# Macaron block in one pipelined kernel: the first channel mix takes x^T from DRAM and normalises it by columns, in a new instruction order

## What is computed

```python
x = x + 0.5 * channel_mix(layernorm(x))      # FFN1
x = x + retention(layernorm(x))              # RET, 8 heads of 32, state carried over the tokens
x = x + 0.5 * channel_mix(layernorm(x))      # FFN2, the same weights

def channel_mix(x):
    x_prev = x shifted by one token, zero in front
    xr = mu_r * x + (1 - mu_r) * x_prev
    xk = mu_k * x + (1 - mu_k) * x_prev
    return sigmoid(xr @ W_r) * (relu(xk @ W_k) ** 2 @ W_v)
```

## Time and profile before

| | us |
|---|---|
| median of 3 runs (lowest, highest) | 339.76 (339.11, 339.87) |
| the profiled execution's own time | 338.8 |
| its span in the trace | 336.9 |
| TensorE busy | 322.3 |
| VectorE busy | 297.0 |
| ScalarE busy | 210.5 |
| GpSimd busy | 135.1 |

### The profile page before, as it was taken

One profiled execution on the slowest core, in us unless ns is written; L12 is line 12 of the kernel. 1 busy time (PEld: TensorE's weight loads), 2 busy tenths in 40 slices (PEclk: granted clock), 3 DMA queues, 4 the chain that ended last, 5 costly groups with the idle time before them and its releaser, 6 DMA issues.

```text
span 336.9 us, 11291 instructions
## 1 busy us (share of the span) xinstructions
PE 322.3 (96%) x4260; PEld 302.4 (90%) x4260; DVE 297.0 (88%) x696; ACT 210.5 (62%) x422; POOL 135.1 (40%) x242
## 2 busy tenths in 40 slices
PE   4979999999999999999999999999999999999975
PEld 4869899999999999999899999989999998989874
DVE  4989899999999999899999989999897979888954
ACT  2877556775757586674758567475857555374362
POOL 4386165608163451706245270715424154221130
PEclk9999999999999999999999999999999999999999
DMA  7610010102001020201102020100000010000001
GB/s 232 247 35 31 4 34 0 34 5 62 4 2 63 2 65 3 65 2 27 41 3 64 2 63 2 53 16 32 2 19 17 2 35 7 26 4 31 34 2 62
DMA packets 11556, 12.08 MB, mean 36 GB/s; under 512 B 1008, under 2 KB 11120, under 8 KB 11504
## 3 DMA queue, kind: packets, MB, share of 16 engines
q1 hardware_dynamic: 11072, 11.18, 10.4%
q10 hardware_dynamic: 432, 0.20, 0.2%
HBM read 7.18 MB, written 4.19 MB: 34 GB/s over the span
## 4 chain that ended last, share of the span: by engine, by line
PE 88%; DVE 4%; issue 3%; ACT 2%; POOL 1%; DMA 1%; ACTq 0%; DVEq 0%; POOLq 0%
PE psum L964 39%; PE psum L956 24%; PE psum L948 7%; PE psum L1035 5%; PE psum L1067 5%; PE psum L1054 3%; PE psum L1025 2%; PE psum L1080 2%; PE psum L1157 1%; DMA ident<-in_ident 1%; ACT xn L344 1%; DVE stats L624 1%; PE psum L1161 1%; PE psum L1127 1%; PE psum L1115 0%
## 5 line engine op out<-in xcount | busy, mean ns | idle before, releaser
L199 POOL TENSOR_TENSOR xr_lo<-xrT,xr_hi 128x512 fp32r<-128x512 f32 x24 | 41.1, 1728 | 99.8 <-ACT xr_hi L375 99.8
L344 ACT ACTIVATE xn<-x,shift,rstd 128x256 f32<-128x256 f32 x96 | 52.0, 591 | 10.1 <-POOL shift L283 10.1
L692 DVE TENSOR_TENSOR attn<-psum,decay 128x512 f32<-128x512 f32 x64 | 42.4, 683 | 4.7 <-PE psum L1035 4.7
L964 PE MATMUL psum<-w_hi,xr_hi 128*128 128x256 f32 x124 | 38.6, 312 | 1.7 <-DVE xr_lo L199 1.2
L624 DVE BATCH_NORM_STATS2 stats<-x 128x6 f32<-128x256 f32 x96 | 35.7, 414 | 4.9 <-DMA x<-in_x 4.6
L276 POOL TENSOR_TENSOR var_eps<-moments,eps 128x2 f32<-128x2 f32 x48 | 18.9, 395 | 43.7 <-DVE moments L628 42.9
L964 PE MATMUL psum<-w_hi,ka_hi 128*128 128x256 f32 x120 | 35.7, 297 | 0.7 <-ACT rgate L403 0.7
L956 PE MATMUL psum<-xa_hi,w_hi 128*128 128x256 f32 x128 | 35.8, 280 | 0.0
L956 PE MATMUL psum<-xk_hi,w_hi 128*128 128x256 f32 x120 | 34.5, 288 | 1.1 <-POOL xk_lo L193 0.9
L956 PE MATMUL psum<-xa_lo,w_hi 128*128 128x256 f32 x128 | 35.5, 278 | 0.0
L956 PE MATMUL psum<-xa_hi,w_lo 128*128 128x256 f32 x128 | 35.5, 277 | 0.0
(11 more groups left out here) (105 smaller groups left out, 1043.4 us busy)
## 6 DMA issues: line engine op xcount, KB each, us to landing
x<-in_x SPq DMA_DIRECT2D x15, 256.0 KB, 2.9
x_out<-y SPq DMA_DIRECT2D x15, 256.0 KB, 3.1
w_f<-in_w SPq DMA_DIRECT2D x7, 256.0 KB, 5.9
decay<-in_decay SPq DMA_DIRECT2D x1, 512.0 KB, 6.6
decq<-in_decq SPq DMA_DIRECT2D x1, 256.0 KB, 6.1
deck<-in_deck SPq DMA_DIRECT2D x1, 256.0 KB, 6.2
x_out<-y SPq DMA_DIRECT2D x2, 128.0 KB, 1.8
x<-in_x ACTq DMA_DIRECT2D x1, 128.0 KB, 2.8
```

The source lines that it names most:

```text
L199: engine.tensor_tensor(xr_lo[f][n % 2][:], xrT[f][n % 2][:], xr_hi[f][n % 2][:].bitcast(F32), ALU.subtract).then_inc(xr_lo_ready[f], 1)
L344: act.activation(xn[s][n % 2][:, t, :], x[n % len(x)][:, t, :], ACT.Identity, bias=shift[s][n % 2][:, t:t + 1], scale=rstd[s][n % 2][:, t: ...
L692: dve.tensor_tensor(attn[r][:], bank[B_SCORES[r]].rearrange("p (g c i) -> p g c i", g=G, c=TILES), decay[:, r, :, :].unsqueeze(2).broadcas ...
L964: mm = pe.matmul(halves(b)[:, t, :], xt[:, g, cols], wt[:, g, :], start=(j == 0), stop=(j == 5))
```

## The change

From block 3 on (`FIRST_ROWS`), the first mix no longer transposes. The host hands over x^T (256 x 4096) as a further input. Per block, SP loads a 256x256 piece of it into `xT` (two buffers), with channels on partitions. `rstd` and `shift` now lie side by side in `scale_shift`, per token on the partitions. SP stores them to a DRAM scratch, 16 bytes for each of 128 partitions, and loads all 512 numbers of the block back into every partition (`rows`, 2 KB each). GpSimd multiplies `xT` by the row of `rstd` and adds the row of `shift`, two operations of 128x512, in place in `xnT`.

```diff
+            def load_xT(n):
+                k = n - FIRST_ROWS
+                sp.wait_ge(xT_scaled, max(k - 1, 0))
+                sp.dma_start(xT[n % 2][:], xT_groups[:, :, n * BT:(n + 1) * BT]).then_inc(xT_loaded[n % 2], 16)
+
+            def store_rows(n):
+                sp.wait_ge(shift_ready[FFN1], shifts(FFN1, n + 1))
+                sp.dma_start(rows_blocks[n], scale_shift[FFN1][n % 2][:].rearrange("p k t -> p (k t)")).then_inc(rows_stored[n % 2], 16)
+
+            def load_rows(n):
+                k = n - FIRST_ROWS
+                sp.wait_ge(rows_stored[n % 2], 16 * stored_rows(n))
+                sp.wait_ge(xnT_ready[FFN1], FIRST_ROWS + k - 1 if k > 1 else 0)
+                sp.dma_start(rows[n % 2][:].rearrange("q p k t -> q (p k t)"), rows_io[2 * n * BT:2 * (n + 1) * BT].partition_broadcast(P)).then_inc(rows_loaded[n % 2], 16)
...
+            def by_token(row):
+                return row.rearrange("q p t -> q t p").unsqueeze(1).broadcast_to([P, G, TILES, P])
+            def scale_xT(n):
...
+                pool.tensor_tensor(tokens(xnT[FFN1][n % 2][:, :, 1:BT + 1]), tokens(xT[n % 2][:]), by_token(rows[n % 2][:, :, 0, :]),
+                                   ALU.mult).then_inc(xT_scaled, 1)
+            def shift_xT(n):
+                pool.wait_ge(xT_scaled, n - FIRST_ROWS + 1)
+                normal = tokens(xnT[FFN1][n % 2][:, :, 1:BT + 1])
+                pool.tensor_tensor(normal, normal, by_token(rows[n % 2][:, :, 1, :]), ALU.add).then_inc(xnT_ready[FFN1], 1)
```

`dT` is not formed for these blocks. ScalarE scales the block by mu (`scale_k` into `akT`, `scale_r` into `arT`, two operations of 128x256 each), and VectorE adds (1 - mu) * x_prev in the operation it had:

```diff
+            def scale_k(f, n):
+                halo(f, n)
...
+                for g in range(G):
+                    act.activation(akT[n % 2][:, g, :], xnT[f][n % 2][:, g, 1:BT + 1], ACT.Copy, scale=mu[:, 1, g:g + 1]).then_inc(ak_ready, 1)
...
+                if f == FFN1 and n >= FIRST_ROWS:
...
+                    for g in range(G):
+                        dve.scalar_tensor_tensor(out=xkT[f][n % 2][:, g, :], in0=xnT[f][n % 2][:, g, 0:BT], scalar=mu_rest[:, 1, g:g + 1],
+                                                 in1=akT[n % 2][:, g, :], op0=ALU.mult, op1=ALU.add).then_inc(xk_ready[f], 1)
+                    return
```

Three blocks (FFN1 0, RET 0, FFN2 15: `FAST`) are normalised by VectorE as (x - mean) * rstd, and of `inverse_std` only the power stays on GpSimd:

```diff
+            def normalize_fast(s, n, x):
+                dve.wait_ge(rstd_ready[s], n + 1)
+                dve.wait_ge(xnT_psum[s], max(n - 1, 0))
+                for t in range(TILES):
+                    dve.tensor_scalar(xn[s][n % 2][:, t, :], x[n % len(x)][:, t, :], moments[s][n % 2][:, t, 0:1],
+                                      rstd[s][n % 2][:, t:t + 1], ALU.subtract, ALU.mult).then_inc(xn_ready[s], 1)
```

The warm-up reads a tile of zeros, set by GpSimd, in place of `ident`. The PSUM banks are assigned anew, two score masks of `attn` lie in weight buffers that are free by then, and all five lists are in a new order:

```diff
-        B_T = {FFN1: 6, RET: 1, FFN2: 0}
-        B_HID, B_GATE, B_OUT = {FFN1: 7, FFN2: 2}, {FFN1: 2, FFN2: 7}, {FFN1: 5, FFN2: 7}
+        B_T = {FFN1: 7, RET: 4, FFN2: 7}
+        B_HID, B_GATE, B_OUT = {FFN1: 0, FFN2: 3}, {FFN1: 6, FFN2: 3}, {FFN1: 6, FFN2: 7}
...
-            warm_up(3, 14)
+            warm_up(2, 12)
             transpose_T(FFN1, 0)
-            warm_up(3, 13)
+            warm_up(2, 7)
```

More of the change, by code:

```diff
@@ L182, in span, with shifts, stored_rows @@
             return slice(0, G) if part is None else slice(part, part + 1)
+        FAST = {(FFN1, 0), (RET, 0), (FFN2, 15)}
+        def shifts(s, n):
+            return sum((s, k) not in FAST for k in range(n))
+        def stored_rows(n):
+            return max((n - FIRST_ROWS) // 2 + 1, 0)
         def splits(f, n):
@@ L308, in _ @@
+            xr_low(pool, FFN1, 3)
             inverse_std(RET, 2)
-            xr_low(pool, FFN1, 3)
-            inverse_std(FFN1, 5)
+            inverse_std(FFN1, 6)
+            scale_xT(5)
+            xk_low(pool, FFN2, 0)
+            xr_low(pool, FFN2, 0)
+            shift_xT(5)
+            inverse_std(FFN2, 1)
             xk_low(pool, FFN1, 4)
             xr_low(pool, FFN1, 4)
-            inverse_std(FFN2, 1)
-            xr_low(pool, FFN2, 0)
             inverse_std(RET, 3)
-            for i in range(6, 16):
+            for i in range(7, 16):
+                scale_xT(i - 1)
@@ L317, in _ @@
                 inverse_std(FFN1, i)
[L318 to L323 removed]
+                xr_low(pool, FFN2, i - 6)
+                shift_xT(i - 1)
+                inverse_std(FFN2, i - 5)
+                xr_low(pool, FFN1, i - 2)
+                inverse_std(RET, i - 3)
+            scale_xT(15)
@@ L324, in _ @@
+            xr_low(pool, FFN2, 10)
+            shift_xT(15)
+            inverse_std(FFN2, 11)
+            xr_low(pool, FFN1, 14)
+            inverse_std(RET, 13)
+            xr_low(pool, FFN2, 11)
             inverse_std(FFN2, 12)
-            add_ffn(pool, FFN1, 14)
-            square_low(pool, FFN1, 15)
             inverse_std(RET, 14)
-            add_ffn(pool, FFN2, 11)
+            xk_low(pool, FFN2, 12)
             add_ffn(pool, FFN1, 15)
@@ L794, in _ @@
-            gate(FFN1, 3)
-            decayed_query(2)
-            add_retention(1)
             add_ffn(dve, FFN1, 3)
-            layer_stats(FFN2, 1, x2)
+            decayed_key(2)
             layer_stats(RET, 3, x1)
-            decayed_key(2)
-            for i in range(6, 16):
-                layer_stats(FFN1, i, x0)
-                square_low(dve, FFN2, i - 6)
+            mask_scores(1, 2)
+            update_state(0, 2)
+            mask_scores(3, 2)
+            scale_state(1, 2)
@@ L1251, in _ @@
+            scores(1, 2, first=True)
+            scores(1, 3)
+            scores(1, 1)
+            scores(1, 0, last=True)
+            pe.wait_ge(krow_ready, 2)
+            outer(1)
+            pe.wait_ge(q_ready, 2)
             hidden(FFN1, 3, 0)
             hidden(FFN1, 3, 1)
-            pe.wait_ge(krow_ready, 2)
-            outer(1)
+            pe.wait_ge(val_ready, 2)
+            transpose_T(FFN2, 0)
+            pe.wait_ge(attn_ready[3], 2)
+            gate(FFN1, 3, 0)
+            gate(FFN1, 3, 1)
```

1100 lines of the change are left out of this document (593 added, 507 removed).

## The result

The changed kernel takes 343.43 us (median of four runs, 342.40 to 344.60), the kernel before beside it 339.44 (338.98 to 339.87). The ratio is 1.0119, 95% interval 1.0083 to 1.0155: 1.2% slower, where 1.8% faster was forecast. The profiled execution has a span of 341.7 us instead of 336.9.

What follows compares the result with a forecast made beforehand. It took TensorE's own work to bound the rounds. Transposes -5.7, start -0.3 and end -0.3 summed to -6.3 us, giving a median of 333.5 us from 339.76, range 330.0 to 338.8.

Steps and rivals of the forecast that it cites:

- Point 1: First mix, blocks 3 to 15: 13 sets of four transposes leave TensorE at 0.44 us each, saving 5.7 us.
- The forecast's own test: Ten rounds: a round of 18.9 to 19.0 us shows it right; above 19.2 us the forecast falls.
- Points 2 and 3: Rounds: VectorE loses one difference, 17.63 us; ScalarE swaps normalisation and copy for four scalings, 13.5 us, hidden.
- Point 4: Rounds: GpSimd gains two 128x512 operations per block, 1.28 us each, at worst 2.31; its round becomes 10.5 us.
- Point 5: SP's queue: x^T load plus row store and load, the latter two taking 5 to 12 us, stay hidden.
- the margin of 0.7 us: Rounds: the moved load of x lands after 3.0 us, while statistics need it after 3.7 us.
- Point 6: Start: first transposes move from 7.90 to about 8.6 us; in all -0.3 us, between -1.5 and +1.5.
- Point 7: End: last transposes come 0.5 us earlier, last gate ends 0.2 later; in all -0.3 us, between -1.5 and +1.0.
- The sign that it gave for being wrong: End: the estimate is wrong if the last transposes lie less than 12.7 us before the end.
- C: Rounds: a wait for x, a mask or `relu` replaces the transposes, 2 to 4 us back: 335.5 to 339.0, chance 0.16.
- D: Start and end gain more, 1.5 us from each: 328.5 to 331.5 us, chance 0.08.
- B: Rounds: VectorE and GpSimd block each other, deciding from 1.33 us per round: 342 to 346 us, chance 0.11.

Runs made afterwards that it cites:

- run 6: The realigned kernel with TensorE kept busy at the start by 22 instead of 12 warm-ups and 26 keep-warm matmuls: 335.98 us, ratio 0.9915.
- realigned kernel: The changed kernel with 32 unused bytes behind `zeros`, so the moved tiles start at multiples of 64 bytes again: 338.58 us, ratio 0.9971.
- Run 9: run 6 with `xr_low(FFN2, 14)` on VectorE and 4 instead of 18 keep-warm matmuls before the last transposes: 333.49 us, ratio 0.9817.
- run 8: The realigned kernel with `w_lo` of W_V and `xr_lo` of (FFN2, 14) moved from GpSimd to VectorE: 338.30 us, ratio 0.9991.
- run 5: The realigned kernel with the retention's set of four transposes done twice in each of the ten rounds: 344.19 us, ratio 1.0152.

## Why the prediction was wrong, by its steps

**Point 1 (13 sets) was right, and something else hid it.** With the placement undone, the round is 18.92 against the forecast 18.96. The step that failed is the unspoken one: all other matmuls would keep their distance of 0.12. They went from 0.116 to 0.119, 0.32 us per round (19.24 - 18.92), and 4.9 us of the medians (343.43 to 338.58). Nothing in the sum had a term for where the tiles lie, though the diff shows that tiles are added. The forecast's own test ("falls if the round is above 19.2") struck at 19.24. With the placement alone undone, the median of 338.58 is still 5 us above the forecast: points 6 and 7 failed as well, in their size.

**Points 2 and 3 were right.** VectorE's round is 17.67 (forecast 17.63) where GpSimd does not hold it up, ScalarE's 13.08 (13.5); a scaling takes 0.50, not 0.54.

**Point 4: the size was off, without effect.** The new operations take 1.56 us instead of 1.28, inside the bounds of 1.28 to 2.31; GpSimd's round is 11.07 instead of 10.5. The traces don't tell how much of the 0.28 is the stepped, repeated operand. It called the places free of VectorE operations on two SBUF inputs "except a `scale_state` of 0.13". That exception is the `state_dec` above, and it cost VectorE 1.3 us (1.55 - 0.21) in four of ten rounds.

**Point 5 was right.** x^T lands after 2.7 us, the rows 1.9 + 3.4 after the store's issue (medians), and GpSimd waits for neither. Behind the start no statistics wait for x, so the margin of 0.7 us held.

**Point 6 was wrong by 4.8 us** (35.06 against 30.3). It let the first normalisation wait for the statistics of block 1 alone and gave 8.6 for the transposes; they came at 9.23, since the power itself waited for `mu` until 7.46 behind `mu_rest`. Of TensorE's idle warm-up it said that some work might run at the lower clock, and kept this within 1.5 us. It was the largest part that was found: run 6, which undoes it alone, took 2.6 us from the realigned kernel's median. The second pause, 22.46 to 25.85, was not in the forecast at all: it counted that two GpSimd steps fall away for the retention's first normalisation, not that 1.1 us of blocking, the statistics and the difference of other blocks come ahead of it.

**Point 7 was wrong by 4.5 us.** It let GpSimd make `xr_lo` of (FFN2, 14) early. GpSimd waited 7.54 us for `xr_hi` and began at 320.92, beside VectorE's operations, and held `xk_lo` up. Run 9 gives back 2.3 of it, 0.9 is placement (83.32 - 82.47), and 1.4 remain in the new order of the end (80.15 against 78.8), which was not tried apart. The sign that it gave for being wrong did not strike: the last transposes lie 13.0 us before the end (341.7 - 328.71), not under 12.7. The time was lost ahead of them, where the sign did not look: they come 17.25 us after the last scores instead of 14.26.

**The rivals.** C and D did not happen. 343.43 lies in B's 342 to 346, by accident. B's mechanism did happen: in four of the ten rounds, where `state_dec` is held, and at start and end, with the operations at 20 us and at 321 among others. But in the rounds it stayed within what VectorE had free. The 1.3 us is just what B named as deciding (1.33) against a round of 18.96; the realigned kernel's rounds stayed at 18.92, with VectorE busy for up to 18.48 of them. That VectorE and GpSimd block each other where a VectorE operation has two SBUF inputs and GpSimd's reads SBUF is what the Trainium skill says ("SBUF — State Buffer", the section on the two separate sides); the trace agrees, with 1.84 for 0.75, 1.76 for 0.69 and 1.55 for 0.21. But it is not what made the kernel slower: without the two at 20 and 321 us, the end of run 8 is 0.8 us shorter and its median is not told apart. The slowdown of 4.0 us is 4.9 from the placement and 2.6 from TensorE's pauses, against some 3 us that the rest of the change gains. These are medians of three series, in which the kernel before had 339.44, 339.01 and 338.84. The last term is therefore known only roughly: 3.5 by the first series (339.44 - 335.98), 2.9 by that of run 6 (338.84 - 335.98).

## What to carry to other kernels

Where TensorE is the bound, compare the distance of its matmuls before and after, not their duration, and look at the addresses of both operands as soon as a tile is added: here 32 bytes decided between 1.2% slower and none. Where an order is written by hand, read for each engine what stands ahead of the first operation on the path; a small one that waits for a late load (`mu_rest`) costs as much as a large one. A pause of TensorE of 3 us costs twice, once itself and once in the clock behind it, so price both, and bridge it with matmuls that end just before the work comes; more than that delays it, as the 18 at the end did.

## What the runs showed of the hardware

- In these kernels, fp32r matmuls of 128x128 by 128x256 follow each other by 0.1160 to 0.1162 us in the mean when both operands start at a multiple of 64 bytes in the partition, or both 32 bytes past one, and by 0.1186 to 0.1191 when one does and the other doesn't. Only 0 and 32 were tried, so the period isn't known. Placement is not all: with operands that lie alike, the mean was 0.1169 in run 5, and the keep-warm matmuls kept 0.120. In the kernel before, the loss by placement was stronger for products with the weight stationary (0.1199 against 0.1177), in the changed one for the others (0.1183 against 0.1197); this stays open.
- After TensorE had stood still for 3.2 and 3.4 us, 3.8 to 4.2 us of work had a mean granted clock of about 0.6. In run 8, pauses of 2.04 and 1.58 us close together were followed by 4.3 us at 0.50. Kept busy, it stayed at 1.00.
- A second set of four transposes of 128x128 took 0.44 us in its place, as the rows had shown. The round grew by 0.55, since other matmuls slowed too, and shrank by 0.48 when a set was left out (with the new order).
- A VectorE operation on two SBUF inputs of 0.21 us took 1.55 beside a GpSimd operation of 1.57 that had begun 0.10 us earlier.
